# A graph-attention kernel: channel halves across heads, one score product in place of two, and a staggered prologue

## The reference

```python
h = (x @ W.T).reshape(n, H, D)
h_src = h[src]; h_dst = h[dst]
alpha = einsum('ehd,hd->eh', h_src, a_src) + einsum('ehd,hd->eh', h_dst, a_dst)
enc = relu(edge_attr @ edge_W.T + edge_b).reshape(-1, H, D)
alpha = alpha + sum(enc * h_dst, axis=-1)
alpha = where(alpha >= 0, alpha, 0.2 * alpha)
ex = exp(alpha - segment_max(alpha, dst)[dst])
attn = ex / max(segment_sum(ex, dst)[dst], 1e-10)
out = segment_sum(h_src * attn[..., None], dst)
```

## Time and profile before

| | |
|---|---|
| median of 3 runs | 6731.35 us |
| the profiled execution | 6730.72 us |
| its span, first to last instruction | 6728.6 us |
| mean granted clock of PE | 0.887 of full speed |
| busy: PE, DVE, ACT, POOL | 4888.9, 3264.7, 1365.0, 3649.6 us |
| share of the span | 73%, 49%, 20%, 54% |
| first edge stage, first gather to last copy out | 243.9 to 2568.8 us |

### The profile page before, as it was taken

The page is one execution under the profiler, slowest core; times in us unless marked ns, Lnnn a source line. Parts: engine busy times, 40 slices in busy tenths (PEclk is TensorE's granted clock), DMA queues, the critical chain, the costliest instruction groups (busy, mean ns, idle before and its releaser), DMA issues. The chain is left out here.

```text
span 6728.6 us, 99218 instructions
## 1 busy us (share of the span) xinstructions
PE 4888.9 (73%) x19729; PEld 3527.3 (52%) x19729; DVE 3264.7 (49%) x5938; ACT 1365.0 (20%) x2977; POOL 3649.6 (54%) x3708
## 2 busy tenths in 40 slices
PE   1689999999999992359999625656565655643698
PEld 0245555555555551359999514444444444433698
DVE  6556666666666666311111324444454444445244
ACT  1322222222222220112222201111011111101122
POOL 1667777777777750332222067777777777711322
PEclk9899999999999996579999858888888888875899
DMA  6555555555555546146666555555555555533455
GB/s 218 178 137 157 153 153 155 156 153 156 154 154 155 156 117 216 42 147 181 181 183 186 155 127 142 139 139 139 139 141 138 143 136 142 138 99 120 163 199 190
DMA packets 718013, 1022.24 MB, mean 152 GB/s; under 512 B 301733, under 2 KB 531561, under 8 KB 692608
## 3 DMA queue, kind: packets, MB, share of 16 engines
q0 software_dynamic: 183456, 485.95, 27.7%
q1 hardware_dynamic: 527676, 519.31, 25.3%
q10 hardware_dynamic: 6564, 14.14, 0.6%
HBM read 868.26 MB, written 153.27 MB: 152 GB/s over the span
## 5 line engine op out<-in xcount | busy, mean ns | idle before, releaser
L773 POOL DMA_INDIRECT e_rows<-sc_table,e_eidx x3224 | 3152.7, 978 | 1140.3 <-issue 974.0
L872 PE MATMUL e_ps_o<-e_rows,e_oh 128*128 128x264 f32 x6448 | 1665.2, 403 | 288.8 <-ACT e_res L963 147.6
L872 PEld LDWEIGHTS e_ps_o<-e_rows,e_oh 128*128 128x128 f32 x6448 | 1214.2, 196 | 747.8 <-issue 573.1
L1126 DVE TENSOR_TENSOR e_rows<-e_rows,e_ps_w 128x1024 f32<-128x1024 f32 x806 | 970.2, 1206 | 7.8 <-ACT e_rows L956 3.5
L1058 DVE SCALAR_TENSOR_TENSOR e_u<-e_encr,e_adst,e_ps_hd 128x512 f32<-128x512 f32 x806 | 593.3, 744 | 659.2 <-PE e_ps_X L822 467.4
L822 PE MATMUL e_ps_X<-e_u,e_hwide 128*104 128x512 f32 x1612 | 812.7, 597 | 16.4 <-DVE e_u L1058 16.2
L963 ACT COPY e_res<-e_ps_o 32x264 f32<-32x264 f32 x806 | 296.2, 367 | 2483.5 <-PE e_ps_o L876 2057.7
L1670 PE MATMUL x_ps_h<-x_xT,x_w 128*128 128x256 f32 x2624 | 647.3, 405 | 13.9 <-DMA x_b<-in_L_ffn_b_dram 13.9
L1670 PEld LDWEIGHTS x_ps_h<-x_xT,x_w 128*128 128x128 f32 x2624 | 638.0, 337 | 18.6 <-issue 14.8
L1681 PE MATMUL x_ps_y<-x_w,x_hT 128*128 128x256 f32 x2624 | 579.9, 379 | 0.0
L936 ACT ACTIVATE e_encr<-e_ps_enc 128x512 f32<-128x512 f32 x806 | 475.9, 590 | 370.2 <-PE e_ps_enc L810 369.4
(11 more groups left out here) (290 smaller groups left out, 4057.6 us busy)
## 6 DMA issues: line engine op xcount, KB each, us to landing
x_w<-in_L_ffn_W_dram SPq DMA_DIRECT2D x112, 1024.0 KB
e_at<-sc_grp SPq DMA_DIRECT2D x403, 192.0 KB
x_w<-in_L_ffn_w_dram SPq DMA_DIRECT2D x60, 1024.0 KB
e_rows<-sc_table,e_eidx POOLq DMA_INDIRECT x3224
e_at<-sc_grp SPq DMA_DIRECT2D x403, 96.0 KB
sc_agg<-e_res SPq DMA_DIRECT2D x816, 33.0 KB
sc_xb<-r_zero SPq DMA_DIRECT2D x24, 1032.0 KB
x_xin<-sc_xb SPq DMA_DIRECT2D x86, 258.0 KB
```

Of the source, the lines that this page charges most:

```text
L773: pool.indirect_dma_start(rows[:, k, s, j, :], None, dr["table"][:, :], bass.IndirectOffsetOnAxis(eidx[:, k, s, j:j + 1], 0)).then_inc(s_r ...
L872: nc.tensor.matmul(ps_o[:, 0:ROW], oh[:, k, at_j:at_j + P], rows[:, k, s, j, :], start=(j == 0), stop=False)
L1126: nc.vector.tensor_tensor(part, part, ps_w[:, k, :, s * HEADS:(s + 1) * HEADS].unsqueeze(3).to_broadcast([P, CH, HEADS, DH]), ALU.mult).th ...
```

## The change

The two halves of the channels are cut another way. Before, half 0 held heads 0 to 3 and half 1 heads 4 to 7. Now each half holds 16 channels of every head. So partition p of half 0 and partition p of half 1 belong to the same head, and the two products can be added element by element before the heads are summed. DVE does that addition (new L1075, `u = ps_u + ub`), with one product in PSUM (`ps_u`) and one in SBUF (`ub`), and PE does one score product for a group in place of two (L829).

To lay out the halves, ACT's and DVE's instructions in the node stage read or write in the new channel order (L466 and L523), `w_rest` takes one more small copy, and `a_dst` is loaded by 16 small DMAs in place of one. `ps_u` needs a PSUM bank, so `ps_s` is given up: the transposes of the batch's chain go to unused columns of `ps_w` (`flat(k)`).

The prologue is staggered: PE does `score` of group s-2 between the two `enc` of group s, as the loop does already, and DVE builds `ohT` of the next group ahead of the products of this one.

```diff
-                    nc.scalar.copy(hp[:, k, 0, :], ps_h[:, t % 2, 0:D]).then_inc(s_p0, 1)
+                    nc.scalar.copy(hp[:, k, 0, :].rearrange("p (h g d) -> p g h d", h=2, g=HEADS),
+                                   ps_h[:, t % 2, 0:D].rearrange("p (g h d) -> p g h d", h=2, g=HEADS)).then_inc(s_p0, 1)
...
-                nc.vector.tensor_tensor(hr[:, k, :], row[:, k, 0:D], hp[:, k, 0, :], ALU.subtract).then_inc(s_r1, 1)
+                side = lambda part: part.rearrange("p (h g d) -> p h g d", h=2, g=HEADS)
+                nc.vector.tensor_tensor(side(hr[:, k, :]), row[:, k, 0:D].rearrange("p (g h d) -> p h g d", h=2, g=HEADS), side(hp[:, k, 0, :]),
+                                        ALU.subtract).then_inc(s_r1, 1)
...
-            u = sb("u", [P, 2, 2, G], F32)
+            u = sb("u", [P, 2, G], F32)
+            ub = sb("ub", [P, G], F32)
+            ps_u = ps("ps_u", [P, 512])
...
-        ps_s = ps("ps_s", [P, 512])
...
-        CF, PH = 2 * COLS, 2 * COLS + 2
+        CF, PH = 3 * P + COLS, COLS
+        flat = lambda k: ps_w[:, k, :, :].rearrange("p j c -> p (j c)")
...
-                    sp.dma_start(adst[:, :], io["L0_gnn_a_dst"].rearrange("(k g) d -> (g d) k", k=2)).then_inc(s_w, 16)
+                    for g in range(HEADS):
+                        for k in range(2):
+                            sp.dma_start(adst[g * (DH // 2):(g + 1) * (DH // 2), k:k + 1],
+                                         io["L0_gnn_a_dst"][g:g + 1, k * (DH // 2):(k + 1) * (DH // 2)].rearrange("a d -> d a")).then_inc(s_w, 16)
...
-            def score(b, s, h, last):
-                if last:
-                    hold(pe, s_u, (b * SB + s) * 2 + (h + 1), s_pp)
-                nc.tensor.matmul(ps_X[0:COLS, :], hwide[:, h, COLS - HEADS * (s + 1):2 * COLS - HEADS * (s + 1)], u[:, par(s), h, :],
-                                 start=(s == 0 and h == 0), stop=False, skip_group_check=True).then_inc(s_xa, 1)
+            def score(b, s):
+                hold(pe, s_us, b * SB + (s + 1), s_pp)
+                nc.tensor.matmul(ps_X[0:COLS, :], hwide[:, COLS - HEADS * (s + 1):2 * COLS - HEADS * (s + 1)], u[:, par(s), :],
+                                 start=(s == 0), stop=False, skip_group_check=True).then_inc(s_xa, 1)
...
-            def scores(b, s):
-                if s == 0:
-                    free_scores(b)
-                if not first:
-                    score_owner(b, s)
-                    return
-                enc(b, s, 0)
-                enc(b, s, 1)
-                score(b, s, 0, True)
-                score(b, s, 1, True)
+            def products(b):
+                for s in range(SB):
+                    if s == 2:
+                        free_scores(b)
+                    if first:
+                        enc(b, s, 0)
+                        if s >= 2:
+                            score(b, s - 2)
+                        enc(b, s, 1)
+                    elif s >= 2:
+                        score_owner(b, s - 2)
+                if first:
+                    for s in range(SB - 2, SB):
+                        score(b, s)
...
-                        for h in range(2):
-                            enc(n, s, h)
-                            if s >= 2:
-                                score(n, s - 2, h, False)
+                        enc(n, s, 0)
+                        if s >= 2:
+                            score(n, s - 2)
+                        enc(n, s, 1)
...
             def products(b, s, p):
                 t = b * SB + s
+                if not isinstance(t, int) or t >= 1:
+                    hold(v, s_us, t, s_pv)
                 for h in range(2):
                     hold(v, s_relu, t * 2 + (h + 1), s_pv)
                     hold(v, s_hd, t * 2 + (h + 1), s_pv)
-                    if not isinstance(t, int) or t >= 2:
-                        hold(v, s_xa, t * 2 + (h - 3), s_pv)
-                    nc.vector.scalar_tensor_tensor(u[:, p, h, :], encr[:, h, :], adst[:, h:h + 1], ps_hd[:, h, :],
+                    nc.vector.scalar_tensor_tensor((ps_u if h == 0 else ub)[:, :], encr[:, h, :], adst[:, h:h + 1], ps_hd[:, h, :],
                                                    ALU.add, ALU.mult).then_inc(s_u, 1)
+                hold(v, s_u, t * 2 + 2, s_pv)
+                if not isinstance(t, int) or t >= 2:
+                    hold(v, s_xa, t - 1, s_pv)
+                nc.vector.tensor_tensor(u[:, p, :], ps_u[:, :], ub[:, :], ALU.add).then_inc(s_us, 1)
...
             for s in range(SB):
+                if s + 1 < SB:
+                    owners(0, 0, s + 1, (s + 1) % 2)
                 if first:
                     products(0, s, s % 2)
-                if s + 1 < SB:
-                    owners(0, 0, s + 1, (s + 1) % 2)
```

More of the change, by code:

```diff
@@ L622, in edge_phase @@
         s_ei, s_ns, s_fr, s_rows = ([sem(f"{n}{k}") for k in range(2)] for n in ("ei", "ns", "fr", "rows"))
-        s_nid, s_dn, s_oht, s_enc, s_hd, s_relu, s_u, s_xa = (sem(n) for n in ("nid", "dn", "oht", "enc", "hd", "relu", "u", "xa"))
+        s_nid, s_dn, s_oht, s_enc, s_hd, s_relu, s_u, s_us, s_xa = (sem(n) for n in ("nid", "dn", "oht", "enc", "hd", "relu", "u", "us", "xa"))
         s_X, s_y, s_lk, s_f, s_b, s_turn, s_q, s_f8, s_mr, s_mc, s_al, s_d, s_col, s_phi, s_phb, s_cf, s_m = (
@@ L846, in logits, with turned, columns @@
                 mm.then_inc(s_X, 1)
-            def turned(b):
+            def turned(b, k):
                 hold(pe, s_b, b + 1, s_pp)
-                nc.tensor.transpose(ps_s[0:1, 0:COLS], bmax[:, 0:1], ident[0:COLS, 0:COLS])
-                nc.tensor.transpose(ps_s[0:1, COLS:2 * COLS], bmax[:, G - 1:G], ident[0:COLS, 0:COLS]).then_inc(s_turn, 1)
-            def columns(b):
+                nc.tensor.transpose(flat(k)[0:1, 0:COLS], bmax[:, 0:1], ident[0:COLS, 0:COLS])
+                nc.tensor.transpose(flat(k)[0:1, COLS:2 * COLS], bmax[:, G - 1:G], ident[0:COLS, 0:COLS]).then_inc(s_turn, 1)
+            def columns(b, k):
                 hold(pe, s_mc, b + 1, s_pp)
                 for n in range(2):
-                    nc.tensor.matmul(ps_s[0:COLS, CF + n:CF + n + 1], mcol[0:1, n, :], one[0:1, 0:1], start=True, stop=True)
+                    nc.tensor.matmul(flat(k)[0:COLS, CF + n:CF + n + 1], mcol[0:1, n, :], one[0:1, 0:1], start=True, stop=True)
                 hold(pe, s_phi, b + 1, s_pp)
-                nc.tensor.matmul(ps_s[:, PH:PH + HEADS], one[0:1, :], phi[0:1, :], start=True, stop=True).then_inc(s_col, 1)
+                nc.tensor.matmul(flat(k)[:, PH:PH + HEADS], one[0:1, :], phi[0:1, :], start=True, stop=True).then_inc(s_col, 1)
             def weights(b, k):
@@ L893, in phase @@
                     if turn and s == 4:
-                        turned(m)
+                        turned(m, 1 - k)
                     if turn and s == 7:
-                        columns(m)
+                        columns(m, 1 - k)
                     if turn and s == 10:
@@ L901, in phase @@
                         if first:
-                            score(n, s, 0, True)
-                            score(n, s, 1, True)
+                            score(n, s)
                         else:
@@ L907, in _ @@
             par = lambda s: s % 2
-            for s in range(SB):
-                scores(0, s)
+            products(0)
             logits(0)
-            turned(0)
-            columns(0)
+            turned(0, 0)
+            columns(0, 0)
             weights(0, 0)
             par = lambda s: (SB + s) % 2
-            for s in range(SB):
-                scores(1, s)
+            products(1)
             steps = steps_of(pe)
@@ L1022, in _ @@
             if first:
-                done(nc.vector.memset(hwide[:, :, :], 0.0))
+                done(nc.vector.memset(hwide[:, :], 0.0))
                 done(nc.vector.memset(w_enc[:, :], 0.0))
-                done(nc.vector.tensor_copy(hwide[:, :, COLS - HEADS:COLS], hmask[:, :, :]))
+                done(nc.vector.tensor_copy(hwide[:, COLS - HEADS:COLS], hmask[:, :]))
                 v.sem_inc(s_ready, 1)
-                v.wait_ge(s_w, 48)
-                done(nc.vector.tensor_copy(w_part[:, 0, :], w_st[:, :]))
-                done(nc.vector.tensor_tensor(w_rest[:, :], w_st[:, :], w_part[:, 0, :], ALU.subtract))
+                v.wait_ge(s_w, 16 * (2 + 2 * HEADS))
+                done(nc.vector.tensor_copy(w_rest[:, :].rearrange("q (h g d) -> q g h d", h=2, g=HEADS), w_st[:, :].rearrange("q (g h d) -> q g h d", h=2, g=HEADS)))
+                done(nc.vector.tensor_copy(w_part[:, 0, :], w_rest[:, :]))
+                done(nc.vector.tensor_tensor(w_rest[:, :], w_rest[:, :], w_part[:, 0, :], ALU.subtract))
                 done(nc.vector.tensor_copy(w_part[:, 1, :], w_rest[:, :]))
@@ L1118, in carried @@
                 nc.vector.tensor_tensor(cs[0:WIN, 0:D].rearrange("p (h c) -> p h c", h=HEADS), res[0:WIN, last, 0:D].rearrange("p (h c) -> p h c", h=HEADS),
[L1119 to L1120 removed]
```

(4 more changed lines are left out.)

31 lines of the change are left out of this document (16 added, 15 removed).

## The result

The changed kernel takes 6768.66 us in the median (6763.49 to 6782.3, 6 runs), the kernel before 6730.57 (6 runs beside it): ratio 1.006, 95% interval 1.0047 to 1.0073. The forecast was 6610 us, with a range of 6575 to 6668.

The account below looks back on a forecast made before the run. POOL was to bound the first edge stage's loop at 68.0 + 0.56 us a batch; with the prologue's wait gone the last gather came 120.9 us sooner, in all -121.6 us on 6730.7: 6610 us, range 6575 to 6668.

Parts of the forecast that it names:

- Part 2: First edge stage's loop: the addition costs DVE 0.84 us a group, 10.9 us a batch, raising it from 47.8 to 58.7.
- worst case: Loop: all 10 us of DVE's once-a-batch work delay PE, added to its 60.3 us: 70.3 us a batch.
- The first rival: Loop: DVE and PE wait for each other, period 69.5 to 71 us, 6659 us at 70.3; chance 0.25.
- Part 1: Loop: one score product less a group saves PE 11.2 us a batch, from 71.5 to some 60.3 us.
- about 0.2 us a group: Loop: the slack to which DVE and PE waiting for each other would fall, from over 1.5 us in each group.
- Part 3: Loop's gathers on POOL: the addition, with one input in PSUM, does not slow them; the mean stays 1003 ns.
- the rival built on it: Loop: the addition shuts POOL out, 9.0 us a batch more, 77.6 us a batch, 6870 us; chance 0.06.
- the sign of being wrong: Loop: a mean gather moved by over 20 ns would show the claim that the addition leaves gathers at 1003 ns wrong.
- the rival of cheaper gathers: Loop: gathers lose part of their 47 ns above the second stage's mean, period 67 us, 6563 us; chance 0.08.
- Part 4: Prologue: staggering its groups removes POOL's wait for PE's first sum, 31.9 us saved.
- Part 5: Small things: 16 small DMAs delay the gathers 0.6 us (bounds 0 and 4); node stage's subtraction 0, at worst 10 us.
- The slower case: Loop: one SBUF input suffices for the addition to lock POOL out, +139 us, 6870 us; chance 0.06.

Follow-up runs that it names:

- the first experiment: The kernel before with only the prologue's groups staggered, loop and score products unchanged: 7716.55 us, ratio 0.9953 to the kernel before.
- the lead: The changed kernel with DVE scaling the gathered rows two groups ahead of PE's sum instead of one, first edge stage: 7817.41 us, 0.9939 of the kernel before.
- a product of zeros: The changed kernel with one more 512-column PE product with zero weights in 11 of 13 groups a batch: 7844.91 us, 0.9966 of the kernel before.

## Why the prediction was wrong

- **Part 2 failed**, in the sentence "I take it that some 5 to 7 us are, which gives 65 to 67 us: just hidden behind POOL". Its worst case, all 10 us added to PE's 60.3, had the waits about right (8.2 us were added to the idle time). What it had no term for is what PE does after such a wait: 5.5 us a batch lost at half clock, and 1.2 us that stay open. 71.4 - 11.2 + 8.2 + 5.5 + 1.2 = 75.1; with the 8.2 alone this balance would give 68.4, the forecast's own period. The first rival named the clock ("once it pauses, can also lose clock") and priced it at nothing; its band of 69.5 to 71 ended 4 us short.
- **Part 1** was right in what it removes (the group's score products fell from 507.5 / 19.6 = 25.9 to 254.7 / 18.63 = 13.7 us a batch). The 11.2 us did not stay saved: 5.5 went to the clock. Not POOL, but PE and DVE in turn set the period.
- **Part 2's own price**: 692 ns as taken; the wait for the product ahead was 67.0 / 242 = 0.28 us where 0.15 was taken. 0.97 us a group instead of 0.84, 1.7 us a batch. That ate most of the slack of "about 0.2 us a group".
- **Part 3** was right on the addition: the mean gather is 971 ns, not longer than 1003, so the addition doesn't shut POOL out, and the rival built on it is dead. But "1003 ns stays" was not right. The mean moved by 32 ns, more than the 20 that I had set as the sign of being wrong, and down, as in the rival of cheaper gathers; why is open. It had no effect here, since POOL is not the bound.
- **Part 4 held** in its mechanism: the wait is gone, confirmed alone by the first experiment.
- **Part 5**: I took the 1.99 us as the price of the one strided DMA, to be saved. But the first of the 16 small ones takes 1.995 us in its place, and the other 15 take 0.42 us each, not 0.30: 3.8 us late instead of 0.6, inside the bound of 4 that I had named and not used. For the node stage's subtraction, half as much again of 745 ns is 0.37 us and 49 of them 18 us, not 10; it took 738 ns, so nothing came of it. The second edge stage did not move.
- **The slower case** was looked for in the wrong place. I gave 0.06 to a lock that the rows spoke against, and no room above 71 us to the pair that they spoke for, DVE's once-a-batch work and PE's clock, although the second stage's clock of 0.86 stood in the earlier trace rows.

Shown: the pauses and the half clock behind them (trace of the first chip); and on the other chips, that the lead removes the sum's pauses and brings 71 to 74 us against the changed kernel, and that a product of zeros brings 46 us. Argued from the profile only: that on the first chip the loss splits in the proportion 8.2 to 5.5, and that the addition is what makes the scaled rows late there. Open: whether a PE with fewer products loses clock on the first chip even without these pauses, as it did on another chip when the addition was left out; what lengthens the edge stages on the other chips, how large the addition's own share is, and what the lead would bring on the first chip.

## What to carry to other kernels

Work taken from the busiest engine is a gain only while that engine stays fed: ask which instructions of the engine that takes the work over stand ahead of what the first one waits for next, and move those ahead (a second buffer's lead) in the same change. On TensorE price each new pause like these of some 2 us twice, once as it is and once as the half clock behind it. Where mean slack a group falls to tenths of a microsecond, count the once-a-batch work group by group instead of adding it to a mean.

## What the runs showed of the hardware

- After one pause of 2.54 us PE ran at 1.2 GHz for the next 4.7 us of unbroken work; eight products took 3.86 us instead of 1.98.
- A PE product that computes nothing made the kernel faster, by 46.2 us of 7891, while the granted clock over the span rose from 0.828 to 0.842.
- Without one of two score products a group and without the addition, the loop took as long as with both products (2580.8 and 2584.2 us), at a granted clock of 0.825 against 0.855 over the span.
- A DVE instruction that reads what the one just ahead of it wrote started 0.28 us behind it in the mean of 242.
- Of 16 DMAs of 16 channels each that SP issued in a row, the first took 1.995 us and the others 0.42 us; the one strided DMA that they replace had taken 1.99.
